# Two small fp32 matmuls per image, split into column halves, in a per-image convolution kernel

## The chip, the cores and the metric

The kernel runs on one core of a Trainium2 chip. The metric is the device time of one execution in microseconds. The kernel before was run three times.

## The reference

Each of 16 images (32 channels, 96 x 96, fp32) is normalised per channel. A softmax over its channel means mixes seven expert kernels into one kernel of its own for each of two 3x3 convolutions. The result is added to the normalised image and to the input.

```python
def _gn(v, G=32, eps=1e-05):
    g = v.reshape(B_, G, C_ // G, H_, W_)
    m = jnp.mean(g, axis=(2, 3, 4), keepdims=True)
    s = jnp.var(g, axis=(2, 3, 4), keepdims=True)
    return ((g - m) / jnp.sqrt(s + eps)).reshape(v.shape)
...
identity = x
pooled = x.mean(axis=(-2, -1))
gate = jax.nn.softmax(pooled @ gate_w.T + gate_b)
kw1 = jnp.einsum('be,eoihw->boihw', gate, experts_w1) + conv1_w
kb1 = gate @ experts_b1 + conv1_b
kw2 = jnp.einsum('be,eoihw->boihw', gate, experts_w2) + conv2_w
kb2 = gate @ experts_b2 + conv2_b
out1 = jax.nn.relu(per_sample(x, kw1, kb1))
out2 = per_sample(out1, kw2, kb2)
return identity + out2 * RES_SCALE
...
x = x + _L0_conv_ref(_gn(x), ...)
```

## The kernel before

An image lies in `img` as 128 partitions: 32 channels times 4 interleaved rows (row 4k+g is on partitions 32g to 32g+31). The convolutions run in fp16 in three products (high by high, high by low, low by high). Each is done by two sets of matmuls that write the two halves of the same PSUM tile `pg`: one set has "straight" weights and image, the other "crossed" ones, in which the lower and the upper 64 partitions are exchanged. Every convolution matmul contracts 128 partitions and has 64 output columns (128x64 at the array); `products` (L384) alternates the sides, so that neighbours write different halves. A convolution has five groups of 18 matmuls (L390), nine pairs.

The round of an image s on TensorE (L464) is: conv1 groups 0 to 3 of s, `gather_rows` of s+2, conv1 group 4 of s, conv2 groups 0 and 1 of s-1, `logits` of s+2, conv2 groups 2 to 4 of s-1. Six rounds form the body of a hardware loop that runs twice; the rest is unrolled.

`gather_rows` (L370) is the first small matmul: it waits until VectorE has this image's means and variances in `triples`, and sums and spreads them over the four row groups by multiplying with the 128x128 matrix `same`, 12 columns, into `pstat`. VectorE's `channel_moments` (L625) waits for it. `logits` (L377) is the second: `ones` (128x128) times `gwp`, 7 columns, into `pgate`, for the softmax. Both are fp32.

VectorE's round (`slot`, L802, a list like TensorE's) mixes the weights of image s+1 (`mixture`, L653, eight steps); the first step stands ahead of `channel_moments` of s+2, the others behind it, with the low parts of the hidden image (`hidden_low`, L688) between them. `weights` (L673) ends it. SyncE's queue (L320) then sends, in this order: the load of image s+2, the crossed weights (`cross_weights`, L305, two transfers between the partition halves), the stores of s-2 and the crossed image of s+1. conv1 group 0 of the next round waits for the crossed weights (L407).

Of the kernel before, what the change touches and what calls it, by code (L numbers as in the profile page):

```python
# [35 lines left out]
P = 128  # L36
# [54 lines left out]
def build(nc, x, w1, b1, w2, b2, ew1, eb1, ew2, eb2, gw, gb, out):  # L91
    N, C, H, W = x.shape
    E = ew1.shape[0]
    G = P // C
# [15 lines left out]
    with ctx:  # L110
        def sb(name, shape, dt=F32):
            return ctx.enter_context(nc.sbuf_tensor(name, shape, dt))

        def sem(name):
            return ctx.enter_context(nc.semaphore(name))
# [21 lines left out]
        same = sb("same", [P, P])  # L137
        row = sb("row", [P, 2, G])
        triples = [sb(f"triples{i}", [P, G, 3]) for i in range(2)]
        ones = sb("ones", [P, P])  # L140
# [8 lines left out]
        gwp = [sb(f"gwp{i}", [P, E]) for i in range(RING)]  # L149
# [6 lines left out]
        pstat = ctx.enter_context(nc.psum_tensor("pstat", [P, 512], F32))  # L156
        pgate = ctx.enter_context(nc.psum_tensor("pgate", [P, 512], F32))
# [21 lines left out]
        rows_ps = sem("rows_ps")  # L179
# [6 lines left out]
        gate_ps = sem("gate_ps")  # L186
# [147 lines left out]
        def _(pe):  # L334
# [35 lines left out]
            def gather_rows(t):  # L370

                pe.wait_ge(mv_ok, t.number + 1)
                nc.tensor.matmul(pstat[:, 0:3 * G], same[:, :],  # L373
                                 triples[t.parity][:, :, :].rearrange("p g a -> p (g a)"),
                                 start=True, stop=True).then_inc(rows_ps, 1)

            def logits(t):  # L377
                pe.wait_ge(gwp_ok, t.number + 1)
                if not t.known(0):
                    pe.wait_ge(logit_ok, t.number)  # L380
                nc.tensor.matmul(pgate[:, 0:E], ones[:, :], gwp[t.ring][:, :],
                                 start=True, stop=True).then_inc(gate_ps, 1)

            def products(v, s, g, pairs, *sides):  # L384
                for image, weight in pairs:
# [62 lines left out]
            for n in range(8):  # L448
                transpose_kernels(n)
            gather_rows(Sample(0, 0))  # L450
            transpose_table()
            logits(Sample(0, 0))
            gather_rows(Sample(0, 1))
            logits(Sample(0, 1))
            warm_up()
            first_conv1()
            conv1_group(Sample(0, 1), 0)
            gather_rows(Sample(0, 2))
            conv1_group(Sample(0, 1), 1)
            conv1_group(Sample(0, 1), 2)  # L460
            conv1_group(Sample(0, 1), 3)
            logits(Sample(0, 2))

            def slot(s):  # L464
# [468 lines left out]
```

## Time and profile before

| | |
|---|---|
| three runs | 372.33, 370.74, 369.99 us (median 370.74) |
| the profiled execution's own time | 372.14 us |
| its span, first to last instruction | 370.3 us |
| granted TensorE clock, mean | 0.973 |
| TensorE, VectorE, ScalarE, GpSimd busy | 86, 78, 68, 52% |
| DMA | 60.95 MB, mean 165 GB/s |

A row of the time line gives start and length in us, engine, line, operation, output and input, shape at the array (contraction by columns) and count; brackets give how long the engine stood idle ahead of it and what ended that. PE is TensorE's matmul and PEld its weight load. An fp32 matmul leaves two records of each, one for each pass.

### The profile page before, as it was taken

The page shows a single profiled execution, that of the slowest core. Times are in us where ns is not written, and L with a number is a line of the kernel's source. Part 1 is how long each engine was busy: PE and PEld are TensorE (multiplying, and loading weights), DVE is VectorE, ACT ScalarE, POOL GpSimd, SP SyncE. Part 2 cuts the span into 40 slices and gives each one's busy share as a digit, 9 for nine tenths or more (in the row PEclk, how much of TensorE's full clock was granted, in tenths as well). Part 3 has the DMA queues.
Part 4 walks back from the last instruction along what each step waited for, and adds up shares of the span by engine and source line. Part 5 has one row for each costly group of instructions (what it writes and reads, how often), then busy time and mean ns, then how long its engine had stood idle before and what let it go on. Part 6 is the DMA issues. An engine that isn't in the chain of part 4 may idle for free.

```text
span 370.3 us, 8529 instructions
## 1 busy us (share of the span) xinstructions
PE 317.8 (86%) x2983; PEld 199.9 (54%) x2983; DVE 288.6 (78%) x651; ACT 252.7 (68%) x278; POOL 192.8 (52%) x236
## 2 busy tenths in 40 slices
PE   2327673599999998999797899999999989999993
PEld 2316442256565756575554457565657565676552
DVE  4699945688979898898787698989989888693432
ACT  1155219895968787787677587878778787965710
POOL 8039417492828383757547083837475755931000
PEclk9999969599999999999999999999999999999998
DMA  9932920688999798969995888979797996395055
GB/s 196 222 67 60 226 67 2 138 164 201 188 209 199 177 217 188 211 148 211 220 213 133 189 151 183 214 178 212 183 216 169 214 195 132 88 203 141 2 130 129
DMA packets 109387, 60.95 MB, mean 165 GB/s; under 512 B 102944, under 2 KB 105248, under 8 KB 109344
## 3 DMA queue, kind: packets, MB, share of 16 engines
q1 hardware_dynamic: 108544, 59.79, 77.5%
q10 hardware_dynamic: 608, 0.59, 0.6%
q8 instruction: 26, 0.43, 0.5%
q14 instruction: 17, 0.14, 0.1%
q0 software_dynamic: 192, 0.01, 0.0%
HBM read 19.47 MB, written 18.87 MB: 104 GB/s over the span
## 4 chain that ended last, share of the span: by engine, by line
PE 59%; DVE 15%; DMA 9%; issue 7%; SPq 3%; ACT 3%; POOL 2%; ACTq 0%; DVEq 0%; POOLq 0%
PE pg L390 56%; DMA wts<-wts 6%; DVE mix L660 5%; DVE wts L677 3%; DVE a L691 2%; DMA c<-a 2%; PE pg L353 2%; DVE stats L615 2%; PE pstat L373 2%; POOL a L879 1%; SPq L274 1%; DMA natural<-in_L_conv_conv_w 1%; SPq L310 1%; DVE img L707 1%; SPq L301 1%
## 5 line engine op out<-in xcount | busy, mean ns | idle before, releaser
L390 PE MATMUL pg<-a,wts 128*64 128x480 f16 (+1 forms) x1440 | 292.6, 362 | 15.8 <-DMA c<-a 6.0
L390 PE MATMUL pg<-c,wts 128*64 128x480 f16 (+1 forms) x1440 | 298.1, 366 | 0.0
L390 PEld LDWEIGHTS pg<-c,wts 128*64 128x64 f16 x1440 | 154.6, 110 | 70.2 <-issue 1.1
L390 PEld LDWEIGHTS pg<-a,wts 128*64 128x64 f16 x1440 | 155.0, 110 | 51.1 <-issue 12.8
L548 ACT ACTIVATE hid<-pg,col 128x480 f32<-128x480 f32 x80 | 52.5, 657 | 51.6 <-PE pg L390 41.6
L879 POOL TENSOR_TENSOR a<-xh,a 128x576 f16<-128x576 f32 x64 | 79.0, 1267 | 13.0 <-POOL col L887 8.5
L660 DVE SCALAR_TENSOR_TENSOR mix<-bank,gate,mix 128x386 f32<-128x386 f32 x96 | 74.0, 771 | 2.4
L860 POOL TENSOR_TENSOR col<-col,minus_half 128x1 f32<-128x1 f32 x16 | 13.5, 843 | 117.5 <-DVE col L633 117.5
L691 DVE TENSOR_TENSOR a<-hid,a 128x480 f16<-128x480 f32 x80 | 52.5, 657 | 23.1 <-ACT a L548 22.3
L564 ACT COPY c<-a 64x2352 f32<-64x2352 f32 x32 | 68.9, 2153 | 2.1 <-DVE a L691 1.9
L707 DVE SCALAR_TENSOR_TENSOR img<-pg,img 128x480 f32<-128x480 f32 (+1 forms) x80 | 48.1, 633 | 15.4 <-PE pg L390 13.1
L893 POOL TENSOR_SCALAR img<-img,col 128x1152 f32<-128x1152 f32 x32 | 57.9, 1816 | 0.1
L548 ACT ACTIVATE a<-pg,col 128x480 f16<-128x480 f32 x80 | 52.5, 656 | 0.0
L615 DVE BATCH_NORM_STATS2 stats<-img 128x6 f32<-128x384 f32 x96 | 45.6, 545 | 1.0 <-DMA img<-in_x 0.8
L505 ACT ACTIVATE xh<-img,col 128x2304 f32<-128x2304 f32 x16 | 36.9, 2307 | 11.5 <-POOL col L861 11.5
L510 ACT ACTIVATE a<-img,col 128x2304 f16<-128x2304 f32 (+1 forms) x17 | 37.3, 2194 | 6.5 <-POOL col L861 6.5
L677 DVE TENSOR_TENSOR wts<-mix,wts 128x384 f16<-128x384 f32 x16 | 20.6, 1289 | 0.3 <-ACT wts L533 0.3
L373 PE MATMUL pstat<-triples,same 128*128 128x12 f32 x32 | 7.0, 293 | 15.4 <-DVE triples L622 15.4
L533 ACT CAST wts<-mix 128x384 f16<-128x384 f32 x16 | 8.2, 512 | 15.7 <-DVE mix L660 15.7
L373 PEld LDWEIGHTS pstat<-triples,same 128*128 128x128 f32 x32 | 5.5, 215 | 21.4 <-DVE triples L622 16.0
L630 DVE COPY col<-pstat 128x1 f32<-128x1 f32 x16 | 2.5, 158 | 18.6 <-PE pstat L373 18.6
L353 PE MATMUL pg<-ident,padded 128*128 128x128 f32 x24 | 5.6, 424 | 8.7 <-DVE padded L721 8.7
(61 smaller groups left out, 143.5 us busy)
## 6 DMA issues: line engine op xcount, KB each, us to landing
c<-a SPq DMA_DIRECT2D x28, 588.0 KB, 7.1
img<-in_x SPq DMA_DIRECT2D x56, 288.0 KB, 6.9
out<-img SPq DMA_DIRECT2D x60, 180.0 KB, 3.0
out<-img SPq DMA_DIRECT2D x60, 108.0 KB, 2.3
wts<-wts SPq DMA_DIRECT2D x28, 96.0 KB, 2.6
c<-a SPq DMA_DIRECT2D x8, 294.0 KB, 5.9
img<-in_x SPq DMA_DIRECT2D x16, 144.0 KB, 5.1
out<-img SPq DMA_DIRECT2D x4, 120.0 KB, 2.1
```

Of the source, the lines that this page charges most:

```text
L390: last = nc.tensor.matmul(pg[g][side * 64:side * 64 + 64, at:at + nb * W].rearrange("p (b w) -> p b w", w=W), wts[s.c % WSETS][kind][:, v, ...
L505: nc.scalar.activation(xh[t.parity][:, :, :], img[t.ring][:, :, :], ACT.Identity, bias=c[:, NBIAS:NBIAS + 1], scale=c[:, RSTD:RSTD + 1]).t ...
L510: return nc.scalar.activation(a1[t.parity][:, HI, b0:b1, 1:1 + W], img[t.ring][:, b0:b1, :], ACT.Identity, bias=c[:, NBIAS:NBIAS + 1], sca ...
L548: last = nc.scalar.activation(o, pg[g][:, 0:SPG * W].rearrange("p (b w) -> p b w", w=W), ACT.Relu, bias=c[:, B1:B1 + 1], scale=HS / WS)
L564: last = nc.scalar.copy(d, a[:, :, first:first + NB * RP // 2])
L615: last = nc.vector.bn_stats(stats[t.ring][:, j, :], flat[:, j * SC:(j + 1) * SC])
L660: nc.vector.scalar_tensor_tensor(out=mix[:, (e + 1) % 2, :, :], in0=bank[:, e, :, :], scalar=gate[t.ring][:, e:e + 1], in1=bank[:, E, :, : ...
L677: nc.vector.tensor_tensor(st[:, :, LO, :], mix[:, E % 2, :, 0:TAPS], st[:, :, HI, :], ALU.subtract).then_inc(w_ok, 1)
L691: nc.vector.tensor_tensor(a2[s.parity][:, LO, j0:j1, 1:1 + W], hid[g_parity(s, g)][:, :, :], a2[s.parity][:, HI, j0:j1, 1:1 + W], ALU.subt ...
L707: nc.vector.scalar_tensor_tensor(out=r, in0=pg[g][:, 0:(b1 - b0) * W].rearrange("p (b w) -> p b w", w=W), scalar=1.0 / (WS * HS), in1=r, o ...
L879: last = nc.gpsimd.tensor_tensor(a1[t.parity][:, LO, b0:b1, 1:1 + W], xh[t.parity][:, b0:b1, :], a1[t.parity][:, HI, b0:b1, 1:1 + W], ALU. ...
L893: last = nc.gpsimd.tensor_scalar(img[t.ring][:, b0:b1, :], img[t.ring][:, b0:b1, :], c[:, RS1:RS1 + 1], c[:, RB:RB + 1], ALU.mult, ALU.add)
```

## The change

Both small matmuls are done as two, one for each half of the 128 columns of the stationary matrix, into the matching half of the PSUM partitions. The moving operand is the same for both, and the second one alone raises the semaphore. Nothing else changes: the four instructions stand where the two stood.

```diff
             def gather_rows(t):
 
                 pe.wait_ge(mv_ok, t.number + 1)
-                nc.tensor.matmul(pstat[:, 0:3 * G], same[:, :],
-                                 triples[t.parity][:, :, :].rearrange("p g a -> p (g a)"),
-                                 start=True, stop=True).then_inc(rows_ps, 1)
+                for h0, h1 in ((0, P // 2), (P // 2, P)):
+                    last = nc.tensor.matmul(pstat[h0:h1, 0:3 * G], same[:, h0:h1],
+                                            triples[t.parity][:, :, :].rearrange("p g a -> p (g a)"),
+                                            start=True, stop=True)
+                last.then_inc(rows_ps, 1)
 
             def logits(t):
                 pe.wait_ge(gwp_ok, t.number + 1)
                 if not t.known(0):
                     pe.wait_ge(logit_ok, t.number)
-                nc.tensor.matmul(pgate[:, 0:E], ones[:, :], gwp[t.ring][:, :],
-                                 start=True, stop=True).then_inc(gate_ps, 1)
+                for h0, h1 in ((0, P // 2), (P // 2, P)):
+                    last = nc.tensor.matmul(pgate[h0:h1, 0:E], ones[:, h0:h1], gwp[t.ring][:, :],
+                                            start=True, stop=True)
+                last.then_inc(gate_ps, 1)
```

## Rows read from the trace of the kernel before

**Rows 1.** The page: busy times, granted clock and DMA share in 40 slices.

```profile
PE 317.8 (86%) x2983; PEld 199.9 (54%) x2983; DVE 288.6 (78%) x651; ACT 252.7 (68%) x278; POOL 192.8 (52%) x236
PEclk9999969599999999999999999999999999999998
DMA  9932920688999798969995888979797996395055
```

**Rows 2.** Waits: who waited for whom, us in total, times, longest.

```profile
DVE col L630 <- PE pstat L373: 18.6, 14, 4.5
PE pg L390 <- DMA wts<-wts: 5.7, 6, 1.9
```

**Rows 3.** Round from 181, its gather matmul: L373's durations (ns), then time line.

```profile
L373 PEld LDWEIGHTS pstat<-triples,same x32: 186/189/338, 18.6 to 308.4; 128*128 128x128 f32 x32
...
188.24 0.37 PE L390 MATMUL pg<-c,wts 128*64 128x480 f16 x1
188.53 0.30 PEld L373 LDWEIGHTS pstat<-triples,same 128*128 128x128 f32 x2 [0.39 <-issue]
188.53 0.39 PE L373 MATMUL pstat<-triples,same 128*128 128x12 f32 x2
...
188.85 0.39 PE L390 MATMUL pg<-a,wts 128*64 128x480 f16 x1
188.86 0.39 PE L390 MATMUL pg<-c,wts 128*64 128x480 f16 x1
...
188.88 0.11 PEld L390 LDWEIGHTS pg<-c,wts 128*64 128x64 f16 x1
...
188.96 0.16 DVE L630 COPY col<-pstat 128x1 f32<-128x1 f32 x1 [1.16 <-PE pstat L373]
```

**Rows 4.** Time line of TensorE: around a logits matmul; a gather at low clock.

```profile
194.19 0.36 PE L390 MATMUL pg<-c,wts 128*64 128x480 f16 x1
...
194.80 0.39 PE L390 MATMUL pg<-c,wts 128*64 128x480 f16 x1
...
68.72 0.60 PE L373 MATMUL pstat<-triples,same 128*128 128x12 f32 x2 [9.51 <-DVE triples L622]
```

**Rows 5.** Time line of TensorE: starts of rounds and of gather matmuls.

```profile
101.99 0.34 PE L390 MATMUL pg<-a,wts 128*64 128x384 f16 x1 [0.52 <-DMA wts<-wts]
...
109.46 0.39 PE L373 MATMUL pstat<-triples,same 128*128 128x12 f32 x2
...
128.33 0.39 PE L373 MATMUL pstat<-triples,same 128*128 128x12 f32 x2
...
181.07 0.35 PE L390 MATMUL pg<-a,wts 128*64 128x384 f16 x1 [1.95 <-DMA wts<-wts]
...
202.00 0.34 PE L390 MATMUL pg<-a,wts 128*64 128x384 f16 x1 [1.87 <-issue]
...
242.44 0.35 PE L390 MATMUL pg<-a,wts 128*64 128x384 f16 x1 [0.62 <-DMA wts<-wts]
```

**Rows 6.** Time line of SyncE's queue: the two transfers that cross the weights.

```profile
117.61 1.17 SPq L310 DMA_DIRECT2D wts<-wts  x2
```

**Rows 7.** DMA traffic in 40 slices: windows 238.3:242.5, 117.5:121.5, 156.6:160.6, 277.4:281.4, 315:320.5.

```profile
GB/s 230 223 216 216 227 183 194 198 194 212 212 208 216 205 205 223 234 227 216 183 161 220 205 201 209 136 132 106 59 15 29 15 29 15 0 0 0 0 40 179
...
GB/s 238 207 219 215 219 211 192 177 161 138 111 69 65 223 230 246 154 131 66 127 223 219 204 219 62 31 15 31 0 0 0 0 0 0 0 0 0 0 0 0
...
GB/s 200 223 184 154 146 142 108 96 84 84 115 62 31 108 138 269 227 196 112 39 142 265 230 184 154 93 0 0 0 0 0 0 0 0 0 0 0 0 0 0
...
GB/s 196 192 223 207 211 211 200 161 142 131 96 92 84 177 311 219 207 188 96 115 158 242 215 230 93 31 15 0 0 0 0 0 0 0 0 0 0 0 0 12
...
GB/s 0 0 0 0 0 0 0 0 0 0 0 0 0 0 0 0 0 0 78 223 201 179 34 145 201 201 157 11 0 0 0 0 0 0 0 0 0 0 98 323
```

**Rows 8.** Windows: us; busy us of each engine; clock; DMA share; GB/s.

```profile
128.00:148.00 20.00, 18.76 (x185) 11.70 (x183) 17.34 (x39) 15.48 (x17) 11.75 (x13) 1.00 0.98 201
148.00:167.00 19.00, 19.00 (x188) 11.97 (x185) 17.22 (x39) 15.73 (x18) 11.75 (x13) 1.00 0.87 180
```

## The prediction, made before the changed kernel was run

> **What bounds the kernel now.** I read the page first. TensorE is 86% busy and VectorE 78%; from the ninth slice (74 us) on the granted clock is at its upper level, and the DMA engines are nearly full [rows 1]. No engine is idle for long in the middle, so the question is which path closes each image's round. The waits say it: TensorE waited six times for the crossed weights, and VectorE waited for the statistics matmul (L373) in 14 of 16 images, 18.6 us in total [rows 2]. VectorE is therefore not free of TensorE: the small matmul's result releases it.
>
> Call G the start of an image's statistics matmul in TensorE's stream and T the start of the next round's first conv1 group. From T to G TensorE does four conv1 groups: 181.07 to 188.53, 7.46 us [rows 3, 5]. From G there are two ways to the next T. TensorE's own: one conv1 group, five conv2 groups and the logits matmul. Two undisturbed starts of L373 lie 128.33 - 109.46 = 18.87 us apart [rows 5], so this way is 18.87 - 7.46 = 11.41 us. The other way is the weights': VectorE takes the moments 0.43 us after G, mixes the weights, the queue sends them 8.15 us after G (117.61 - 109.46), the two crossings land, and TensorE starts [rows 5, 6]. It was the later of the two in six rounds: T stood behind "DMA wts" at 101.99, 181.07, 242.44 [rows 5] and in three more rounds, 12.0 to 13.6 us behind G.
>
> In the rounds without such a wait the slack is small. The traffic strips show when the crossed weights' last bytes move. In the reference round they end at 238.3 + 34 slices of 0.105 = 241.87, and TensorE started at 242.44, 0.57 us later [rows 5, 7]. With that 0.57 the weights were ready at 120.87, 159.77, 280.67 and 319.42 in four rounds [rows 7], where TensorE came (the following G less 7.46; for the last, its own G at 308.25 plus 11.41) at 120.87, 160.06, 280.80 and 319.66. The slacks are 0, 0.29, 0.13 and 0.24 us. Three other rounds are TensorE's own: the first, which has the page's low clock just ahead of it, the one in which TensorE stands 1.87 us on "issue" at 202.00 and starts when it has fetched its loop again [rows 5], and the one behind it.
>
> **The change part by part.** Both matmuls move 12 or 7 columns and do the same arithmetic as before. What changes is the shape at the array: 128x128 becomes twice 128x64, the shape of every convolution matmul.
>
> *What one costs now.* Around 188.53 the last convolution matmul starts at 188.24, and the next pair at 188.85 and 188.86 [rows 3]. Within a stream the pairs are about 0.205 us apart, so the small matmul costs 0.61 - 0.205 = 0.41 us; around the logits it is 194.80 - 194.19 - 0.20 = 0.41 [rows 4]. Inside: the last convolution matmul streams until 188.44, then nothing until 188.53 (0.09). Two weight loads of 128 columns take 0.30 us together and one takes 0.19, so the second starts 0.11 behind the first and the pair occupies 0.21. That ends at 188.74, and the next pair starts 0.11 later. The convolution's loads are taken up ahead of time: at 188.88, 0.02 us behind the start of a pair, the load for the next pair starts [rows 3]. The fp32 load is not: it starts with its matmul. So of 0.41 us, 0.20 is standing still at the two changes of shape and 0.21 is loading 256 columns.
>
> *What it will cost.* The four loads of 64 columns are again 256 columns: 0.21 us if they run one after the other. The standing still of 0.20 goes if it belongs to the change of shape. I take both: 0.2 us saved for each small matmul (d = 0.2). The Trainium skill, TensorEngine Tiling (Array Packing), Key Properties, says that changing the tiling mode drains TensorE; the 0.09 and 0.11 us fit it, and are all it could explain of the 0.41. Bounds: at best everything vanishes, because loads of the two halves run at once and beside the stream (d = 0.41); at worst the gaps stay and every pass takes 0.11 whatever its width, so that two more passes add 0.21 (d = -0.21). Issue itself is cheap: two matmuls and the next load start within 0.03 us at 188.85 [rows 3].
>
> *The result's time.* For VectorE only the part before the result counts. The matmul starts 0.09 earlier, and the last pass starts 0.16 behind the first (three loads of 0.053) instead of 0.11 if nothing overlaps, or about 0.05 if the first load is hidden and the halves overlap. I take g = 0.09 as the gain from T to the result, bounds 0.13 and -0.21.
>
> *Where it counts.* The trace counts 32 records of L373, two passes for each of 16 images [rows 3]; L381 has as many. In a round that TensorE itself closes, both matmuls count: 2d. The two rounds around 202 give 4d and the first, which has only its logits matmul in the stream, d: 5 x 0.2 = 1.0 us. In the four rounds with little slack the gain is cut off by the weights: the smaller of 2d = 0.4 and slack + g, so 0.09 + 0.38 + 0.22 + 0.33 = 1.02 us. In the six waiting rounds the logits matmul and everything after G is hidden behind the weights and costs or gives nothing; only g stays. In three of them (12.5 to 13.6 us from G to T) the DMA engines had no room, share 0.98 in 128 to 148 [rows 8], and the weights queued behind images; I give these nothing, and the other three 3 x 0.09 = 0.27 us. The last 50 us have no small matmul. In the start the loads take as many columns as before; nothing.
>
> Sum: 1.0 + 1.02 + 0.27 = 2.3 us. The profiled execution took 372.14 us around a span of 370.3; that should become a span near 368.0. The runs' median is 370.74, so 368.4.
>
> **The rivals.**
>
> *The small matmuls vanish* (0.20). The halves' loads go to separate column halves and ride beside the stream. For it: convolution matmuls of both halves start within 0.01 us of each other and stream together [rows 3]. Against: the second pass of the same half needs its own load behind the first. With d = 0.41, g = 0.13: 5 x 0.41 + (0.13 + 0.42 + 0.26 + 0.37) + 6 x 0.13 = 4.0 us, so 366.7. More is not to be had, because the weights' way from G does not get shorter: if TensorE alone were the bound it would be 28 x 0.41 = 11.5 us.
>
> *No difference* (0.25). The 0.09 and 0.11 us belong to fp32 weights behind fp16 ones, not to the shape, and stay; or the gain is given back to the weights' crossing because the DMA engines, at 0.87 of a round without wait and 0.98 of one with [rows 8], come to be the bound as the rounds get shorter. For it: an 18.87 us round moves nearly the bytes of a longer one. The time stays at 370.7.
>
> *Slower* (0.12). Each fp32 pass costs 0.11 us whatever its width; the matmuls go from two passes to four, and the gaps stay. This is one mechanism, at L373 in the round from T to G, where no slack covers it: 12 rounds x 0.21 = 2.5 us, then 5 x 0.21 = 1.05 for the logits matmul where TensorE closes, and in the four tight rounds 4 x 0.21 = 0.8 again: about 4.3 us, 375.0. It decides once a pass of 64 columns costs over about 0.10 us with the gaps left, for then the result comes later than now. Against it: at 68.72, where the granted clock is low, two passes take 0.60 us instead of 0.39 [rows 4], so their spacing is about twice the warm one and is time of the array, not of a fixed step ahead of it. The Trainium skill, same page, Instruction Overhead, gives about 60 cycles for each matmul and warns not to take a tiling factor from a dimension that is already small, which these 12 and 7 columns are. By its figure two more passes would be an estimated 0.05 us and would leave the sign as it is; no row here shows a 64-column fp32 pass.
>
> **How the numbers follow.** The forecast has 0.43, the rivals 0.20, 0.25 and 0.12. The range 366.3 to 371.7 takes in the first three, with the scatter of the runs before (369.99 to 372.33), and leaves out most of the slower case. About 1% (3.7 us) is what a measurement of this kernel can tell from no change. Faster by over 1% needs nearly everything of the first rival: 0.20. Slower by over 1% is the last rival's upper half: 0.07. Within 1%: 0.73.
>
> **What would show it.** At L373 and L381: four weight loads in place of two, the first of them starting while the last convolution matmul streams, "issue" gone ahead of the loads, and 0.2 us between a pair and the next beyond the stream's 0.205. G to G in a free round near 18.5 us instead of 18.87. VectorE's moments 0.1 us earlier behind T. More or longer waits "DMA wts" on TensorE, since it now reaches them earlier: that is where the rest of the 0.2 us goes. I am wrong if the gaps at the small matmuls stay, if a pass of 64 columns takes as long as one of 128, or if rounds closed by the weights get shorter by more than 0.13 us each.

## The result and the profile after

The changed kernel takes 380.74 us (median of four runs, 377.92 to 383.35) against 370.66 us for the kernel before: 1.026 times as long, 95% interval 1.018 to 1.035. The profiled execution took 381.77 us around a span of 380.0. The forecast was 368.4 us, in a range from 366.3 to 371.7: the kernel became slower where it was foretold to become a little faster. Executions over 1.5% above the fastest of the same kernel are left out of the ratios and medians here and below: one each of e2 and e5, and two of e6's four.

The page, against [rows 1]: engine totals, then granted clock and DMA share in 40 slices.

```profile
PE 315.5 (83%) x3047; PEld 227.0 (60%) x3047; DVE 287.7 (76%) x651; ACT 252.7 (67%) x278; POOL 193.1 (51%) x236
PEclk9956987699999999989996899989998999999998
DMA  9933910989997998997896917999599948386055
```

TensorE is busy 2 us less than before, in a span 10 us longer, and the clock no longer stays up behind the start: it dips in slices of the middle. The waits, against [rows 2]:

```profile
PE pg L394 <- DMA wts<-wts: 16.5, 8, 4.3
DVE col L634 <- PE pstat L374: 15.9, 14, 4.4
PE pg L394 <- issue: 3.4, 1, 3.4
```

TensorE waits 16.5 us for the crossed weights instead of 5.7, and the longest wait is 4.3 us instead of 1.9. VectorE waits 2.7 us less for the statistics matmul.

The split did what was asked of it where it stands. TensorE's time line around the statistics matmul of one round, against [rows 3]:

```profile
187.41 0.14 PEld L374 LDWEIGHTS pstat<-triples,same 128*64 128x64 f32 x1
187.57 0.37 PE L394 MATMUL pg<-c,wts 128*64 128x480 f16 x1
187.61 0.23 PE L374 MATMUL pstat<-triples,same 128*64 128x12 f32 x2
187.70 0.37 PE L394 MATMUL pg<-a,wts 128*64 128x480 f16 x1
187.78 0.37 PE L394 MATMUL pg<-c,wts 128*64 128x480 f16 x1
187.91 0.37 PE L394 MATMUL pg<-a,wts 128*64 128x480 f16 x1
187.98 0.23 PE L374 MATMUL pstat<-triples,same 128*64 128x12 f32 x2
188.06 0.37 PE L394 MATMUL pg<-c,wts 128*64 128x480 f16 x1
...
188.25 0.16 DVE L634 COPY col<-pstat 128x1 f32<-128x1 f32 x1 [0.58 <-PE pstat L374]
```

The fp32 load is now taken up ahead (187.41), and each half sits in its own column half while the other one streams: the side `c` goes 187.57, 187.78, 188.06, so it loses 0.28 - 0.20 = 0.08 us. The small matmul costs 0.08 us instead of 0.41. Rounds that nothing holds up take 18.15 us from gather to gather (257.98 to 276.13) instead of 18.87.

What is lost is lost elsewhere. The rounds of both kernels, from the start of one statistics matmul to the next, in us:

| | 1 | 2 | 3 | 4 | 5 | 6 | 7 | 8 | 9 | 10 | 11 | 12 |
|---|---|---|---|---|---|---|---|---|---|---|---|---|
| before | 21.15 | 19.59 | 18.87 | 20.31 | 18.88 | 21.01 | 22.81 | 18.87 | 19.69 | 19.48 | 18.88 | 19.99 |
| after | 20.10 | 20.11 | 19.31 | 18.95 | 22.79 | 18.47 | 29.02 | 18.22 | 23.13 | 18.15 | 22.80 | 18.48 |

Together 249.5 us against 239.5: the whole loss. 6.2 us of it are in the seventh round, in which TensorE's hardware loop jumps back. The rest comes from rounds of 23 us that now alternate with rounds of 18.2; before, a milder alternation was there already, 18.9 us with 20 to 21. Starts of TensorE's rounds with the idle time ahead of them, against [rows 5]; the third and the fourth row are the two stands of the jump:

```profile
139.34 0.35 PE L394 MATMUL pg<-a,wts 128*64 128x384 f16 x1 [0.58 <-DMA wts<-wts]
160.47 0.35 PE L394 MATMUL pg<-a,wts 128*64 128x384 f16 x1 [2.75 <-DMA wts<-wts]
203.25 0.52 PE L394 MATMUL pg<-a,wts 128*64 128x384 f16 x1 [4.28 <-DMA wts<-wts]
207.30 0.53 PE L394 MATMUL pg<-a,wts 128*64 128x384 f16 x1 [3.43 <-issue]
249.31 0.35 PE L394 MATMUL pg<-a,wts 128*64 128x384 f16 x1 [3.09 <-DMA wts<-wts]
290.25 0.35 PE L394 MATMUL pg<-a,wts 128*64 128x384 f16 x1 [2.73 <-DMA wts<-wts]
```

Windows of after (length; busy us and instructions of PE, PEld, DVE, ACT, POOL; granted clock; DMA share; GB/s): behind the wait of 2.75 us, the jump in two pieces, and two neighbouring rounds.

```profile
160.40:163.80 3.40, 3.33 (x23) 2.41 (x25) 1.19 (x3) 0.05 (x1) 0.00 (x0) 0.62 0.96 244
202.20:207.30 5.10, 0.61 (x3) 0.14 (x3) 2.47 (x6) 0.00 (x0) 0.00 (x0) 0.50 0.77 190
207.30:212.40 5.10, 5.10 (x28) 4.08 (x30) 0.25 (x1) 1.22 (x2) 0.00 (x0) 0.50 0.98 203
...
258.00:276.10 18.10, 18.10 (x190) 12.87 (x188) 16.77 (x39) 15.50 (x17) 11.76 (x13) 1.00 0.74 152
276.10:298.90 22.80, 20.07 (x191) 13.34 (x189) 17.67 (x40) 15.62 (x18) 11.76 (x13) 0.93 1.01 211
```

Behind each of the four long waits the clock is at its lower level (0.50, that is 1.2 GHz), for 3 to 4 us, and at the jump for 10; before, the longest wait, 1.95 us, had no such effect. The way from a round's start to its statistics matmul then takes 169.14 - 160.47 = 8.67 us instead of 146.35 - 139.34 = 7.01:

```profile
146.35 0.23 PE L374 MATMUL pstat<-triples,same 128*64 128x12 f32 x2
...
169.14 0.23 PE L374 MATMUL pstat<-triples,same 128*64 128x12 f32 x2
```

Three such rounds cost 3 x 1.66 = 5.0 us. The jump costs 2.4 us more in its first stand (4.28 for 1.87), 1.75 in its second (3.43 for 1.68) and about 2.6 at the lower clock, less the 0.7 that the split saves. In the other eleven rounds the split takes some 11 x 0.72 = 7.9 us of TensorE's work away, but the waits for the weights grow from 5.7 to 11.8 us and the low clock adds the 5.0. The DMA share of the free round is 0.74 and of the held one 1.01; before, the rounds outside the jump lay between 0.82 and 1.03, so the bunching of the traffic was there and has grown.

### The profile page after: what moved, and what is told of

It reads as the page before. It is cut to its first block, busy times and chain, and to the rows that moved or that the text cites. A ratio compares the mean times of both kernels' runs of the same rounds, so it can differ in the third digit from the quotient of the medians.

```text
span 380.0 us, 8657 instructions
## 1 busy us (share of the span) xinstructions
PE 315.5 (83%) x3047; PEld 227.0 (60%) x3047; DVE 287.7 (76%) x651; ACT 252.7 (67%) x278; POOL 193.1 (51%) x236
## 3 DMA queue, kind: packets, MB, share of 16 engines
HBM read 19.47 MB, written 18.87 MB: 101 GB/s over the span
## 4 chain that ended last, share of the span: by engine, by line
PE 49%; DVE 18%; DMA 14%; issue 9%; SPq 3%; ACT 2%; POOL 2%; ACTq 0%; DVEq 0%; POOLq 0%
PE pg L394 47%; DMA wts<-wts 10%; DVE mix L664 7%; DVE wts L681 4%; DVE a L695 3%; DMA c<-a 2%; DVE stats L619 1%; SPq L310 1%; POOL a L883 1%; DMA natural<-in_L_conv_conv_w 1%; SPq L274 1%; PE pg L353 1%; PE pstat L374 1%; DVE col L635 1%; SPq L301 1%
## 5 line engine op out<-in xcount | busy, mean ns | idle before, releaser
L394 PE MATMUL pg<-a,wts 128*64 128x480 f16 (+1 forms) x1440 | 301.5, 369 | 25.9 <-DMA wts<-wts 16.5
L394 PEld LDWEIGHTS pg<-a,wts 128*64 128x64 f16 x1440 | 159.1, 112 | 71.3 <-issue 16.0
L394 PEld LDWEIGHTS pg<-c,wts 128*64 128x64 f16 x1440 | 156.6, 112 | 39.4 <-issue 1.3
L864 POOL TENSOR_TENSOR col<-col,minus_half 128x1 f32<-128x1 f32 x16 | 13.5, 845 | 126.8 <-DVE col L637 126.8
L374 PE MATMUL pstat<-triples,same 128*64 128x12 f32 x64 | 7.3, 207 | 16.0 <-DVE triples L626 16.0
L374 PEld LDWEIGHTS pstat<-triples,same 128*64 128x64 f32 x64 | 8.2, 152 | 17.4 <-DVE triples L626 16.4
L384 PEld LDWEIGHTS pgate<-gwp,ones 128*64 128x64 f32 x64 | 7.9, 144 | 8.5 <-POOL gwp L874 7.4
```

Source lines behind the costliest of these rows:

```text
L394: last = nc.tensor.matmul(pg[g][side * 64:side * 64 + 64, at:at + nb * W].rearrange("p (b w) -> p b w", w=W), wts[s.c % WSETS][kind][:, v, ...
```

## The experiments

All times are medians; the ratio is to the kernel before, run beside them on the same chip, with its 95% interval. "Low clock" counts the stretches behind 80 us and ahead of 350 in which the granted clock was at its lower level in the profiled execution.

| run | us | ratio | round of the jump, us | low clock |
|---|---|---|---|---|
| kernel before | 370.66 to 371.73 | 1 | 22.81 | 0 |
| changed kernel | 380.74 | 1.026 (1.018 to 1.035) | 29.02 | 4 |
| e1, only the gather split | 370.22 | 0.998 (0.994 to 1.001) | 24.98 | 1 |
| e2, only the logits split | 371.97 | 1.000 (0.997 to 1.003) | 24.88 | 2 |
| e3, changed, filler in the rounds | 369.68 | 0.995 (0.991 to 0.998) | 21.24 | 0 |
| e4, changed, weights from ScalarE's queue | 377.30 | 1.014 (1.012 to 1.016) | 28.79 | 3 |
| e5, before, TensorE's loop written out | 369.00 | 0.995 (0.991 to 0.999) | none | 0 |
| e6, changed, TensorE's loop written out | 367.10 | 0.988 (0.979 to 0.997) | none | 3 |
| e7, before, thin stores | 366.15 | 0.987 (0.981 to 0.993) | 22.39 | 0 |
| e8, changed, thin stores | 371.48 | 1.001 (0.998 to 1.005) | 25.02 | 2 |
| e9, before, eight idle matmuls ahead | 372.61 | 1.005 (1.001 to 1.008) | 25.81 | 1 |
| e10, changed, the same eight | 370.98 | 0.997 (0.994 to 1.001) | 22.81 | 3 |
| e11, changed kernel again | 381.87 | 1.030 (1.023 to 1.037) | 28.16 | 3 |
| e12, e6 with filler | 367.61 | 0.988 (0.981 to 0.995) | none | 0 |
| e13, e6, a quarter of each load later | 363.84 | 0.978 (0.971 to 0.985) | none | 0 |
| e14, e5, the same | 366.68 | 0.988 (0.983 to 0.994) | none | 0 |

### Which of the two, or the time that both save: e1 to e3

e1 takes only the first hunk of the change, e2 only the second. e3 is the changed kernel and

```diff
+            def filler(s, pairs):
+                for _ in range(pairs):
+                    for side in range(2):
+                        nc.tensor.matmul(pset[side * 64:side * 64 + 64, 0:SPG * W], ident16[:, 0:64],
+                                         still[:, 0:SPG * W], start=True, stop=True)
...
                 run(conv2_group, s, -1, 0, 4)
+                run(filler, s, 2, 3, 4)
```

> Only the statistics matmul is split (L373), the logits matmul is whole as before. Theory A (a round that starts early meets weights that are still behind images in the DMA queues; the waits grow over 2.5 us and the clock falls): the round is 0.4 us shorter for TensorE instead of 0.8, so about half of the loss: 373 to 377 us, with one to three waits on the crossed weights over 2.5 us. Theory B (the split gather itself costs, by its late second half): the whole loss, 379 to 382. Theory C (the split logits cost): 370 or less.

> Only the logits matmul is split. Theory A: half of the loss again, 373 to 377 us, with long weight waits, since TensorE reaches the wait 0.4 us earlier. Theory B: 370 to 371, as the gather is untouched. Theory C: 379 to 382.

> The changed kernel with four pairs of convolution-shaped matmuls (0.82 us) into the unused PSUM tile pset at the end of each of TensorE's rounds 1 to 13: this gives back the time that the split saved, just ahead of the wait for the crossed weights. The output is the same. Theory A: the early arrival is the cause, so added work makes it faster: 369 to 373 us, clock back at 0.96 to 0.975, no weight wait over 2.5 us outside the loop's jump. Theories B and C (the split instructions cost where they stand): no better than the changed kernel, 380 or, where TensorE closes rounds, up to 385.

e1: 370.22, e2: 371.97, e3: 369.68 us. Neither half carries the loss (theories B and C fall), and it isn't the sum of the halves either: A wanted 373 to 377 twice. e3 is what A foretold, 11 us faster for 0.82 us of useless work in each round. But its round of the jump fell from 29.0 to 21.2 us, below that of the kernel before, and filler ahead of a wait doesn't explain that. Counting matmuls behind the jump gave the lead. TensorE starts again, runs some, stands again on "issue": in the kernel before it runs 18 convolution matmuls in between, in e1 and e2 10, in the changed kernel 2, and e3 has no second stand at all. The extra split matmuls ahead of the loop (prologue and first round) number 4 in e1 and e2 and 8 in the changed kernel. Each leaves four records more, as much as two convolution matmuls, so 18 - 8 = 10 and 18 - 16 = 2 follow from the length of the program ahead of the loop. TensorE's time line behind the jump, changed kernel and then e1:

```profile
203.25 0.52 PE L394 MATMUL pg<-a,wts 128*64 128x384 f16 x1 [4.28 <-DMA wts<-wts]
203.26 0.61 PE L394 MATMUL pg<-c,wts 128*64 128x480 f16 x1
207.30 0.53 PE L394 MATMUL pg<-a,wts 128*64 128x384 f16 x1 [3.43 <-issue]
```
```profile
199.09 0.34 PE L392 MATMUL pg<-a,wts 128*64 128x384 f16 x1 [1.93 <-issue]
...
199.93 0.37 PE L392 MATMUL pg<-c,wts 128*64 128x480 f16 x1
202.57 0.35 PE L392 MATMUL pg<-a,wts 128*64 128x384 f16 x1 [2.28 <-issue]
```

From the first start to the end of the second stand it is 4.05 us in the one and 3.48 in the other (3.71 before): nearly the same time, with two matmuls done in it or with ten or eighteen.

### Another queue for the weights: e4

The first line leaves SyncE's list, the last one joins ScalarE's, with the same two transfers.

```diff
-                run(cross_weights, s, 0, 2)
...
                 run(high_part, s, 2, 2)
+                run(cross_weights, s, 1, 2)
```

> The changed kernel with the two transfers that cross the weights issued from ScalarE's queue, behind high_part of s+2, instead of SyncE's, so that they don't stand behind the image load in one queue. Theory A: the weights land about 3 us behind their issue also in the crowded rounds, waits fall under 1 us, the clock stays up: 362 to 368 us, faster than both kernels. If the DMA engines as a whole are the limit, not the queue's order: the other transfers are late instead, 372 to 380.

377.30 us, a miss for A. The number lies in the second range, but the other transfers being late was not what showed. Ahead of the jump the rounds did even out (19.99, 18.82, 19.44, 19.34, 19.08 us, waits of at most 1.62), but the jump was as in the changed kernel, with stands of 4.26 and 3.44 us. TensorE's program is the same in both. Behind it the rounds alternated, 18.2 and 23, with waits of 2.87 and 3.18 us, so another queue alone does not keep the weights on time.

### The jump taken out: e5 and e6

```diff
-            schedule(slot, pe, 1, 2, 16)
+            for n in range(1, 17):
+                slot(Sample(0, n))
```

> The kernel before with TensorE's program written out for all 16 rounds, no hardware loop on TensorE; the other engines keep theirs. It had two stands on issue at the loop's end, 1.87 and 1.68 us, 3.5 us beyond a normal round. If they are the loop's: about 3.5 us faster, 366 to 368. If TensorE's program is fetched late anyway: 370 to 372.

> The changed kernel with TensorE's program written out in the same way. Theory D (two thirds of the loss is the loop's end, where the changed kernel stood 4.28 and 3.43 us and then ran 3 us at the lower clock): the round at 188 to 217 falls from 29.0 to about 19.5 us, the time by 8 to 10 us, to 369 to 372, level with its partner. Theory A alone (early arrival at the crossed weights in every round): about 3.5 us as in its partner, 376 to 378, and still 8 us slower than it.

369.0 and 367.1 us; e6's four runs are spread from 365.3 to 372.4. Without the jump on TensorE the two kernels are level within what these runs can tell, as D wanted, and e6 is not 8 us slower, as A alone wanted; e5 gained about 2 us, somewhat less than the 3.5 of the two stands. What A describes stays without the jump: in e6's trace (of its run of 371.22 us) TensorE waits six times for the weights, 1.85 to 2.92 us, and behind three of these waits (2.92, 2.15 and 2.79 us) the clock is low.

### Less traffic: e7 and e8

```diff
-                        sp.dma_start(ov[t.number, g, :, b0:b1, :],
-                                     img[t.ring][g * C:(g + 1) * C, b0:b1, :]).then_inc(stored[t.ring], 16)
+                        sp.dma_start(ov[t.number, g, :, b0:b0 + 1, :],
+                                     img[t.ring][g * C:(g + 1) * C, b0:b0 + 1, :]).then_inc(stored[t.ring], 16)
```

> The kernel before with each store cut to one of its rows for every 9 to 15 (the output is left incomplete: most of it is not written), so that about 1.1 of 3.7 MB of each round's traffic are gone. The weight waits at 101.99, 141.18 and 181.07 should fall away and TensorE close every round at 18.87 us: 362 to 366 us.

> The changed kernel with the same cut of the stores. Theory A (DMA backlog is what makes the early arrival harmful): the split now pays, since there is nothing to wait for: rounds near 18.3 us, 4 to 8 us faster than its partner, 355 to 361, clock 0.97. If the split is harmful without the backlog too (by its place, or by the loop's end alone): slower than its partner by 4 us or more.

366.15 and 371.48 us: with 28% of the traffic gone (43.8 MB instead of 61.0) the split still loses 5.3 us. That is the other way from what A foretold. The jump explains 2.6 us (25.0 against 22.4). And in e8 the waits remained, up to 2.55 us. Traffic of e8 in 40 slices from 153 to 158.5; the weights were issued at 152.89 and TensorE started at 158.45:

```profile
DMA  9999999999999999999999976423000000022003
GB/s 184 212 226 243 293 240 212 218 215 212 204 196 204 212 204 195 212 240 207 315 168 207 204 184 168 123 76 87 11 11 11 11 11 11 11 67 45 6 20 67
```

The engines are full until about 156.3 though hardly anything is stored: this is the crossed image and the load (2.33 MB, issued from 143.06 to 151.6) that stand ahead of the weights in SyncE's queue. The backlog behind which the weights wait is that, not the stores. So e7 and e8 took away the wrong transfers. The last eight of the weights' 128 packets are a part of this wait too: they ended at 157.96, 1.1 us behind the 120th.

### Where the loop starts: e9, e10, and the kernel again, e11

```diff
+            for _ in range(8):
+                nc.tensor.matmul(pset[0:64, 256:264], ident[:, 0:64], ident[:, 0:8], start=True, stop=True)
             gather_rows(Sample(0, 0))
```

> The kernel before, nothing split, with eight idle 64-column fp32 matmuls (8 output columns, into unused columns of pset) ahead of the first statistics matmul, where TensorE waits 4.3 us anyway. They lengthen TensorE's program ahead of its loop by as much as the eight extra split matmuls do there. Theory D2 (where the loop's body starts in the program decides how TensorE comes through the jump): behind the jump TensorE runs 2 matmuls instead of 18 before it stands again, idle times near 4.3 and 3.4 us, the clock falls, the round around 200 takes 27 to 29 us instead of 22.8, the time 375 to 380. Theory A (the early arrival alone): no difference, 370 to 372.

> The changed kernel with the same eight idle matmuls at the same place. Theory D2: the loop's body now starts in another piece of the program, the second stand behind the jump goes away or comes much later, the round around 200 takes about 21 us, as it did with the four filler pairs, and the time is 367 to 371, some 10 us better than the changed kernel for eight instructions that do nothing. Theory A: still 378 to 382.

> The changed kernel itself, unaltered, on the chip and beside the runs of the kernels that follow: 377 to 383 us, with waits for the crossed weights of 2.7 us and more in four rounds, and instruction fetches of 16 KB inside the weights' transfer in those rounds, as in its first profile. If the loss were a matter of one chip, it would be near 371.

The changed kernel takes 381.87 us again, and with eight idle instructions ahead of its loop 370.98: over 10 us for instructions that do nothing. Between the two profiles it is 7.9 us, 5.4 of them in the round of the jump: the second stand is gone and that round takes 22.8 us. The kernel before with the same eight runs 2 matmuls behind the jump and stands again, as foretold:

```profile
199.28 0.34 PE L390 MATMUL pg<-a,wts 128*64 128x384 f16 x1 [2.46 <-POOL a L881]
199.28 0.39 PE L390 MATMUL pg<-c,wts 128*64 128x480 f16 x1
202.27 0.53 PE L390 MATMUL pg<-a,wts 128*64 128x384 f16 x1 [2.60 <-issue]
```

It lost 3.0 us in that round and 1.4 us in the median, less than the 4 to 9 that I expected: its first stand was 2.46 us and not 4.28. The difference is the weights. In the trace of the changed kernel two transfers of instructions, 16 KB each, start at 198.38 and 198.44 and take 2.1 and 2.3 us each, where others take 0.9 to 1.6; of the 32 landings of the weights 30 are there by 200.06 and the last two at 202.43 and 202.73. Traffic of this kernel from 197.4 to 203.4, in 40 slices, and the queue of instructions:

```profile
DMA  9999999864521000047788932020046899889999
...
q8 instruction: 2, 0.03, 4.6%
```

From 199.3 on the engines are nearly idle for 0.6 us and more, with weights still outstanding, so it isn't the amount of traffic that holds the last ones back. In e11 the same pair starts at 196.85 and 197.29, and the last weights' packet at 200.17, 2.6 us behind the 120th of 128. In the changed kernel's first trace the last eight packets start from 200.47 on; five of them took 0.24 to 0.40 us each and the last three 0.07. That the instruction transfers hold up the packets behind them on the same DMA engine fits this; it was not tried by itself. In the other three long waits of both traces a single instruction transfer starts 0.2 to 0.5 us behind the first packet of the weights, and their last packet comes 1.1 to 1.3 us behind the 120th. In the kernel before it was at most 0.5 us, but for the last image's weights, 1.0 us, which met such a transfer too. But it is not the whole of it. In e10 TensorE waited 2.87 us for the weights whose first packet started at 156.76, and their last packet came 0.96 us behind the 120th, though the instruction transfer before them had ended 0.4 us ahead of the first; and in the changed kernel one that overlapped the start of the weights at 117.65 left only 0.1 us between the 120th and the last.

e10 still has three low stretches and alternating rounds, and is therefore level with the kernel before instead of faster. Windows of e10, two rounds:

```profile
166.80:185.10 18.30, 18.29 (x191) 13.67 (x189) 17.00 (x39) 15.52 (x17) 11.75 (x13) 1.00 0.83 175
185.10:207.90 22.80, 19.95 (x190) 14.84 (x188) 17.43 (x40) 15.61 (x17) 11.74 (x13) 0.93 0.96 200
```

### What holds the split's gain back: e12 to e14

e12 is e6 with e3's filler. e13 is e6, and e14 is e5, with

```diff
-                for g in range(G):
+                for g in range(G if early(t) or (isinstance(t.i, int) and t.number < 4) else 3):
                     sp.dma_start(img[t.ring][g * C:(g + 1) * C, :, :],
                                  xv[t.number, g]).then_inc(x_in[t.ring], 16)
...
                 run(cross_weights, s, 0, 2)
+                run(load_rest, s, 2, 4)
```

> The changed kernel with TensorE's program written out for all rounds (no jump, so no place for one) and four pairs of convolution-shaped matmuls, 0.82 us, at the end of rounds 1 to 13, ahead of the wait for the weights. Theory A (in the steady rounds TensorE now arrives too early, waits up to 2.9 us and then runs at the lower clock): waits under 2 us, no drop of the clock behind 80 us, rounds of 18.9 and 20 us instead of 18.2 and 22, and so 2 to 4 us faster than its partner without filler: 366 to 368. If the early arrival costs nothing once the jump is gone: 0 to 3 us slower than it, 370 to 373.

> The changed kernel, TensorE's program written out, and of each image load the last of its four parts (288 KB, 1.4 us of traffic) sent behind the crossed weights instead of ahead. Theory A (the weights land late because they stand behind the image load in the queue): waits in the crowded rounds 1 to 1.5 us shorter, none over 2 us, the clock stays up, and the split's 0.4 to 0.8 us a round are kept: 361 to 366. If the statistics of VectorE, which need that part, come to wait instead: 368 to 374, with VectorE waiting for the image load in most rounds.

> The kernel before with TensorE's program written out and the same last quarter of each load behind the weights. With the weights never late TensorE closes all rounds at 18.87 us: 364 to 367. Theory A wants it slower than the changed kernel in the same form by 2 to 6 us: then the split pays where nothing is waited for.

e12: 367.61 us, no low clock behind 80 us, no wait for the weights over 1.5 us. Added work brings no loss, and the long waits with their low clock are gone. Whether it is faster than e6 these runs don't settle: both ratios are 0.988, with intervals of 0.7 and 0.9%.

e13: 363.84 us (361.0 to 364.7), e14: 366.68 (365.7 to 367.2). Both are faster than the kernel before, and the changed kernel in this form by 2.8 us (0.8%) than the other: with the weights ahead of the last quarter of the load the split pays. Two rounds of e13 and its waits:

```profile
146.40:165.40 19.00, 18.36 (x191) 13.79 (x189) 17.25 (x40) 15.59 (x18) 11.75 (x13) 1.00 0.91 196
165.40:184.40 19.00, 18.45 (x193) 13.78 (x190) 17.11 (x39) 15.40 (x18) 11.74 (x13) 1.00 0.94 206
```
```profile
DVE stats L626 <- DMA img<-in_x: 13.5, 11, 2.2
...
PE pg L400 <- DMA wts<-wts: 9.0, 12, 1.4
```

The rounds are even, 18.8 to 19.6 us with one of 20.6, and the clock is up. Both things that the expectation names came: the weights' waits are short (at most 1.4 us, but 9.0 in total where e14 has 3.5), and VectorE now waits 13.5 us for the late quarter of the images, in e14 as well. So the rounds are 19 and not 18.2, and the gain stayed at 2.8 us, the lower half of what was expected.

## Why the prediction was wrong

- *What a small matmul costs now* (0.41 us, 0.20 of it standing still) was right, and the standing still goes, as foretold. What it costs afterwards was mis-sized: 0.08 us, not 0.21, so d is 0.33 to 0.36 instead of 0.2. The four loads don't run one after the other with the stream standing; each half's load and passes run beside the other half's stream. That was the first rival. The slower rival's warning about small dimensions does not bear on this change: it divides the 128 stationary columns, not the 12 or 7 moving ones.
- *The result's time*, g: from a round's start to VectorE's moments it was 188.96 - 181.07 = 7.89 us [rows 3, 5] and is 146.99 - 139.34 = 7.65, so g is 0.24 us. The rows for it, the second half's passes and the moments:

```profile
146.72 0.23 PE L374 MATMUL pstat<-triples,same 128*64 128x12 f32 x2
...
146.99 0.16 DVE L634 COPY col<-pstat 128x1 f32<-128x1 f32 x1 [0.91 <-PE pstat L374]
```

  My bound of 0.13 had an earlier start and a shorter distance between the passes. The second half starts 7.38 us behind the round's start where the whole matmul started 7.46 behind it, and its two passes take 0.23 us together where those of the whole took 0.39: that second gain was the one I had too small.
- *The two ways from G to T* hold. Free rounds went from 18.87 to 18.15 us, and the rounds behind a free one were held by the weights.
- *"In the six waiting rounds ... everything after G is hidden behind the weights and costs or gives nothing"* is the first step that failed. TensorE arrives 0.7 us earlier at weights that come at most g = 0.24 us earlier, and waiting isn't free: before, the longest wait was 1.95 us and the clock stayed up; in the changed kernel it was at 1.2 GHz behind each of the waits of 2.73 us and more. The length alone does not decide: in e10 the clock fell behind waits of 2.10 and 2.61 us and not behind one of 2.87, in e11 not behind one of 2.55. Each time the next statistics matmul came 1.66 us later than it would have, over twice what the split saves in a round. That the delay also bunches the traffic, and that this is what makes the rounds alternate more, is argued from the DMA shares (0.74 and 1.01) and was not tried. The Trainium skill has the rule for this, TensorE: Matmul & The Clock Gate, HAM oscillation: waits for a transfer in every round let the clock fall and each burst starts cold. The trace of the changed kernel agrees (a granted clock of 0.50 behind each of its four long waits), the traces of e10 and e11 in part, and it was the rule I should have weighed against this change.
- *"The two rounds around 202 give 4d"* is the second, and the larger one. I took the two stands on issue as they were. The first became 4.28 us and the second 3.43, and the clock fell: 6.2 us lost in one round where 0.8 were to be won. How much TensorE does before the second stand depends on where the loop starts in its program, which the eight extra split matmuls ahead of it moved; e9 and e10 show that in both directions. The first stand was longer because the weights landed late there, and why they did is open.
- *The sum* had only terms that could shrink to nothing. The slower rival named another mechanism (a pass that costs 0.11 us whatever its width), which did not occur.

Of the 10 us, 6.2 are the round of the jump and 5.0 the low clock of three further rounds; 1.2 come back, what is left of the saved work when the longer waits are paid. The two parts are not independent: e5, e6, e9, e10 and e11 show that the jump's part decides the sign, since with it set right the same alternation leaves the kernel level with the one before. The jump's part is shown by these runs. The part of the other rounds rests on the time line: e12 has neither the long waits nor the low clock, but its gain over e6 is not settled.

## What to carry to other kernels

An engine that reaches a wait earlier gains nothing from it, and TensorE can lose by it. So when a change shortens TensorE's path, look first at the rounds that already end in a wait, and ask whether the longer wait takes the clock along. Move what it waits for before shortening what it does. And a change of a few instructions ahead of a hardware loop can cost or give several microseconds at its jump, whatever the instructions do: compare kernels with the loop written out, or with idle instructions ahead, before you ascribe a difference to the edit.

## What was not expected of the hardware

- The time from the first matmul behind the jump to the end of the second stand is 3.5 to 4.1 us in the kernel before, e1, e2, the changed kernel and e4, and 2.8 to 3.2 in e7, e8, e9 and e11. How much TensorE does in it, 2, 10 or 18 matmuls, is set by the program's length ahead of the loop, at two convolution matmuls for each half-width fp32 matmul.
- Two fp32 matmuls of 128 x 64 with 12 columns cost the stream 0.08 us where one of 128 x 128 cost 0.41.
- Eight idle matmuls made the changed kernel 10 us faster, and four pairs of idle matmuls in each round did no harm.
